# Decoder of two layers: where the second layer's cross attention gets its tables and first contexts, and the order of two short chains beside it

## The reference, cut to what matters

```python
x = x + L0_attn(ln(x))            # 16 heads, relative bias
x = x + L0_xattn(ln(x), ctx, ctx) # block structured here
x = x + L0_ffn(ln(x))             # 8 experts, two chosen per token, capacity 896 each
x = x + L1_attn(ln(x))            # running sums over the sequence, exp(clip(.)) weights
x = x + L1_xattn(ln(x), ctx)      # 16 heads of 8, rotary, 1500 keys, softmax
x = x + L1_ffn(ln(x))             # 8 routed experts + a shared one
```

```python
logits = xt @ Wg
idx1, idx2 = argmax(gates), argmax(logits without idx1)
pos1 = cumsum(mask1) - mask1, pos2 = cumsum(mask2) - mask2 + sum(mask1)
xe[idx, pos] += xt                                  # dispatch
h = gelu(xe @ W1 + b1); ye = h @ W2 + b2            # experts
out = ye[idx1, pos1] * w1 + ye[idx2, pos2] * w2     # combine
```

## Time and profile before

| | |
|---|---|
| median of three runs | 1534.07 us |
| the profiled execution | 1527.03 us |
| its span in the trace | 1525.2 us |
| TensorE busy | 1358.7 us, 89% |
| VectorE busy | 1093.6 us, 72% |
| ScalarE busy | 821.8 us, 54% |
| POOL busy | 825.7 us, 54% |
| mean granted TensorE clock | 0.951 |
| moved by DMA | 134.71 MB, mean 88 GB/s |

### The profile page before, as it was taken

The page is one execution under the profiler, slowest core; times in us unless marked ns, Lnnn a source line. Parts: engine busy times, 40 slices in busy tenths (PEclk is TensorE's granted clock), DMA queues, the critical chain, the costliest instruction groups (busy, mean ns, idle before and its releaser), DMA issues.

```text
span 1525.2 us, 41823 instructions
## 1 busy us (share of the span) xinstructions
PE 1358.7 (89%) x17179; PEld 927.0 (61%) x17179; DVE 1093.6 (72%) x1832; ACT 821.8 (54%) x1804; POOL 825.7 (54%) x736
## 2 busy tenths in 40 slices
PE   6788999998967996759999999999999999789998
PEld 4567788788935663335666566656665666555554
DVE  6885767656747887747888888888888888435554
ACT  3442334355622331436777777777777777733332
POOL 6665322424654675747778777877787774000000
PEclk9868999999987998779999999999999999989999
DMA  4004400032271034364555554555464554305230
GB/s 128 2 1 128 159 2 2 19 85 86 65 153 39 1 71 78 75 118 124 125 124 133 118 129 123 133 118 132 121 133 118 128 123 93 96 3 111 61 61 13
DMA packets 76511, 134.71 MB, mean 88 GB/s; under 512 B 18017, under 2 KB 56034, under 8 KB 73058
## 3 DMA queue, kind: packets, MB, share of 16 engines
q1 hardware_dynamic: 74274, 127.84, 35.0%
q0 software_dynamic: 2048, 4.20, 1.0%
HBM read 100.54 MB, written 34.73 MB: 89 GB/s over the span
## 4 chain that ended last, share of the span: by engine, by line
PE 35%; POOL 12%; ACT 8%; issue 3%; DVE 3%; DMA 1%; SPq 0%; ACTq 0%; POOLq 0%; DVEq 0%
PE ps L2158 8%; POOL ARENA L2362 8%; PE ps L916 7%; PE ps L2142 5%; POOL ARENA L2368 4%; PE ps L928 4%; PE ps L2105 3%; ACT ARENA L2312 3%; PE ps L2096 2%; ACT ARENA L2290 2%; PE ps L2119 2%; ACT ARENA L2303 2%; ACT ARENA L2296 1%; PE ps L2167 1%; DVE ARENA L2232 1%
## 5 line engine op out<-in xcount | busy, mean ns | idle before, releaser
L2232 DVE TENSOR_REDUCE ARENA<-ps 112x2 f32<-112x1000 f32 x384 | 456.4, 1197 | 122.6 <-PE ps L2119 119.8
L2312 ACT ACTIVATE ARENA<-ps 125x448 f32<-125x448 f32 x768 | 378.4, 549 | 129.0 <-PE ps L2142 128.4
L2362 POOL TENSOR_TENSOR ARENA<-ARENA 64x500 f32<-64x500 f32 x192 | 264.6, 1378 | 106.4 <-ACT ARENA L2290 88.2
L2142 PEld LDWEIGHTS ps<-ARENA 64*125 64x125 bf16 x3072 | 122.9, 134 | 134.6 <-ACT ARENA L2312 70.7
L2142 PE MATMUL ps<-ARENA 64*125 64x112 bf16 x3072 | 169.6, 229 | 19.9 <-ACT ARENA L2312 18.7
L2158 PE MATMUL ps<-ARENA 125*17 125x112 f32 x6144 | 185.5, 261 | 0.0
L2119 PE MATMUL ps<-ARENA 64*112 64x500 bf16 x768 | 153.4, 388 | 9.8 <-DVE ARENA L2232 9.4
L127 POOL TENSOR_TENSOR rs<-rs,mhalf 128x1 f32<-128x1 f32 x96 | 71.7, 750 | 161.1 <-DVE rs L122 160.8
L2158 PEld LDWEIGHTS ps<-ARENA 125*17 125x17 f32 x6144 | 136.7, 97 | 32.1 <-issue 21.9
L2368 POOL TENSOR_TENSOR ARENA<-ARENA 128x500 f32<-128x500 f32 x96 | 147.1, 1533 | 8.1 <-DVE ARENA L2225 0.7
L2373 POOL TENSOR_TENSOR ARENA<-ARENA 128x500 bf16<-128x500 f32 x96 | 111.0, 1157 | 37.7 <-ACT ARENA L2296 37.7
(11 more groups left out here) (273 smaller groups left out, 2384.7 us busy)
## 6 DMA issues: line engine op xcount, KB each, us to landing
ARENA<-key_parts SPq DMA_DIRECT2D x192, 187.5 KB, 3.9
ARENA<-in_ctxT SPq DMA_DIRECT2D x96, 250.0 KB, 3.7
key_parts<-ARENA SPq DMA_DIRECT2D x64, 375.0 KB, 2.6
ARENA<-token_weights SPq DMA_DIRECT2D x16, 512.0 KB, 5.3
slots<-in_c_blank SPq DMA_DIRECT2D x2, 1472.0 KB, 12.5
results<-ARENA SPq DMA_DIRECT2D x42, 64.0 KB, 1.6
ARENA<-in_L_ffn_W SPq DMA_DIRECT2D x1, 2048.0 KB, 8.7
ARENA<-in_L_ffn_W SPq DMA_DIRECT2D x4, 512.0 KB, 10.1
```

Of the source, the lines that this page charges most:

```text
L2142: m = e.matmul(ps[0:KT, b1[h], 112 * g:112 * g + 112], KS[b % 4][r, g, KT * kt:KT * kt + KT], Q1[r, b % 2, 112 * g:112 * g + 112], start=T ...
L2232: e.tensor_reduce(mxp[0:112, b % 2, 2 * g:2 * g + 2, ch], ps[0:112, b1:b1 + 2, 0:500], AX, ALU.max) \
L2312: e.activation(Pb[0:KT, n % NP_, 448 * h:448 * h + 448], ps[0:KT, b1[h], 0:448], ACT.Exp, bias=0.0, scale=1.0).then_inc(exped.sem, 1)
L2362: e.tensor_tensor(T2[r:r + 64, :], T0[64 - r:128 - r, n % 2, :], sin[64 - r:128 - r, sl], ALU.mult) \
```

## The change

Five things change. The long attention's four projection tables, its cosine and sine in three pieces each, and the six pieces of contexts 0 and 1 are issued by SP inside the expert stage, one behind each of the first 16 results. Its other loads (context 2, output weights, the small tables, ones and zeros) are issued in the L1 self-attention once all gathers have landed. For this the arrays of the long attention are laid out anew: contexts, projection tables, cosine and sine between the words of the expert stage and those of the self-attention, context 2 in the last words of the expert stage, and the last stage's arrays begin at the same place. The signal for the early tables (`c0_in`) is apart from that for the rest. On POOL the late norms' powers of a step go to the step's beginning, ahead of its product and its gathers. The second chunk's routing gets a PSUM bank of its own (4), `route` is split (tiles 8 to 14 at expert tile 2, tile 15 at expert tile 3) and goes ahead of `down`, `count` goes ahead of `down` at expert tile 6, and the VectorE parts and the exponential of the gates move one expert tile or more up.

```diff
@@ -1025,6 +1025,7 @@
             REC, NW = 1156, 5
+            R_BANK = (5, 4)
             NI = sum(SLOTS)
...
@@ -1126,37 +1127,44 @@
             def sp(e, w):
+                ahead = stages[4].parts["ahead"]
                 for i in range(NI):
...
                     e.dma_start(YS[c][128 * k:128 * k + 128], Y[:, i % 8]).then_inc(y_out[i % 8].sem, 16)
+                    if i < len(ahead):
+                        ahead[i](e, w)
                     if i == SLOTS[0] - 5:
...
 
-            def route(e, w, c):
+            def route(e, w, c, lo, hi):
+                bk = R_BANK[c]
                 w.wait_ge(*f0_in(len(loads)))
-                w.wait_ge(*free[5])
-                for t in range(*SPLIT[c]):
+                if lo == SPLIT[c][0]:
+                    w.wait_ge(*free[bk])
+                for t in range(lo, hi):
                     w.wait_ge(*ln_out(2, t))
                     n = 8 * (t - SPLIT[c][0])
-                    m = e.matmul(ps[:, 5, n:n + 8], xT[:, 128 * t:128 * t + 128], wg, start=True, stop=True)
-                m.then_inc(routed.sem, 1)
-                free[5] = sel(NSEL * c + 1)
+                    m = e.matmul(ps[:, bk, n:n + 8], xT[:, 128 * t:128 * t + 128], wg, start=True, stop=True)
+                if hi == SPLIT[c][1]:
+                    m.then_inc(routed.sem, 1)
+                free[bk] = sel(NSEL * c + 1)
 
...
                 T = SPLIT[c][1] - SPLIT[c][0]
-                cnt = ps[:, 5, 0:16 * T + 16].rearrange("p (t n) -> p t n", n=16)
+                bk = R_BANK[c]
+                cnt = ps[:, bk, 0:16 * T + 16].rearrange("p (t n) -> p t n", n=16)
                 w.wait_ge(*ones_set(3 + len(Mb) - 1))
...
                 w.wait_ge(*sel(NSEL * c + 14))
-                w.wait_ge(*free[5])
+                w.wait_ge(*free[bk])
                 e.matmul(cnt, trib, Mb[c], start=True, stop=False, skip_group_check=True)
...
                 m.then_inc(counted.sem, 1)
-                free[5] = sel(NSEL * c + 15)
+                free[bk] = sel(NSEL * c + 15)
 
...
@@ -1217,15 +1225,17 @@
                         up(e, w, i)
+                    if i == 2:
+                        route(e, w, 1, SPLIT[1][0], NT - 1)
+                    if i == 3:
+                        route(e, w, 1, NT - 1, NT)
+                    if i == 6:
+                        count(e, w, 1)
                     down(e, w, i - 1)
...
                         ln_turn(e, w, 2, NT - 1, 5, free)
-                    if i == 3:
-                        route(e, w, 1)
-                    if i == 6:
-                        count(e, w, 1)
                     if i in norm_at:
...
@@ -1432,17 +1442,19 @@
             def dve(e, w):
-                steps = {4: ("logits", "first", "second"), 6: ("counts", "bases", "slots"), 7: ("table",), 8: ("gates",), 9: ("shares",)}
+                steps = {3: ("logits", "first", "second"), 4: ("counts", "bases"), 6: ("table",), 7: ("gates",), 8: ("shares",)}
                 for i in range(1, NI + 1):
...
                         ln_scale(e, w, 2, NT - 1)
+                    if i == 5:
+                        choose(e, w, 1, "slots")
                     if i - 2 + NW < NI and i > 1:
...
                         choose(e, w, 1, part)
-                    if i in (10, 11):
-                        keep(e, w, i - 10)
+                    if i in (9, 10):
+                        keep(e, w, i - 9)
                     if i + 1 in norm_at:
...
@@ -1496,7 +1508,7 @@
                         ln_copy(e, w, 2, NT - 1, 5)
-                    if i == 5:
+                    if i == 4:
                         gate(e, w, 1)
...
@@ -1540,7 +1552,7 @@
                          early_pool=early_pool, sp=sp, pe=pe, dve=dve, act=act, pool=pool, gather=gather, combine=combine,
-                         combined=combined,
+                         combined=combined, late=lambda: [g(4) for g in gathered], words=place["used"],
                          end=lambda: [y_cp(NI), down_mm(NI), gated(4 * NI), kept(11), w_cp(NI)] + chunk_out(1))
...
@@ -1786,6 +1798,9 @@
                         stages[2].parts["gather"](e, w, u)
+                    for u in LATE_NORM.get(t - 1, ()):
+                        ln_power(e, w, 3, u)
+                        between.append(ln(INV, 3, u))
                     stages[4].parts["early_pool"](e, w, t, ("total",))
...
@@ -1796,9 +1811,6 @@
                     for u in late[2:] if t == 0 else late:
                         stages[2].parts["gather"](e, w, u)
-                    for u in LATE_NORM.get(t - 1, ()):
-                        ln_power(e, w, 3, u)
-                        between.append(ln(INV, 3, u))
                     if t >= 3:
                         ln_power(e, w, 4, t - 3)
...
@@ -1829,6 +1838,14 @@
             Qh, Ql = mem(TP, BF16), mem(TP, BF16)
+            passing = stages[2].parts["words"] - SK
+            assert place["used"] <= passing
+            place["used"] = passing
+            C = [mem(SK) for _ in range(3)]
+            C = [C[1], C[2], C[0]]
+            wq, wqr, wk, wv = (mem(128) for _ in range(4))
+            cos, sin = mem(SK), mem(SK)
+            assert place["used"] <= ARENA_WORDS - stages[3].parts["words"]
             KSb, Vb = slots(1), values_of(1)
...
@@ -1846,11 +1863,13 @@
             p = "L1_xattn_"
-            loads = [(wq, a[p + "WqT"]), (wqr, a[p + "WqRT"]), (wk, a[p + "WkT"]), (wv, a[p + "WvT"]), (wo, a[p + "WoT"]),
-                     (hm, a["c_own"]), (cos, a["c_cos"]), (sin, a["c_sin"]), (cq, a["c_cosq"]), (sq, a["c_sinq"])]
+            tables = [(wk, a[p + "WkT"]), (wv, a[p + "WvT"]), (wq, a[p + "WqT"]), (wqr, a[p + "WqRT"])]
+            tables += [(v[:, 500 * ch:500 * ch + 500], a[n][:, 500 * ch:500 * ch + 500])
+                       for ch in range(3) for v, n in ((cos, "c_cos"), (sin, "c_sin"))]
+            loads = [(wo, a[p + "WoT"]), (hm, a["c_own"]), (cq, a["c_cosq"]), (sq, a["c_sinq"])]
             ones = lambda dst, r: (dst[r:r + 16].rearrange("p i g k -> p (i g k)"), a["c_ones"][:, 0:dst.shape[1] * 4 * SK])
             loads += [x for r in (48, 112) for x in (ones(KSa, r), (QS[r:r + 16].rearrange("p g n -> p (g n)"), a["c_zero"]))]
-            c1_in, c2_in = signal("c1_in", len(loads), 16), signal("c2_in", 2, 16)
+            c0_in, c1_in, c2_in = signal("c0_in", len(tables), 16), signal("c1_in", len(loads), 16), signal("c2_in", 2, 16)
             qs_in = [signal("qs_in%d" % i, 6, 16) for i in range(2)]
...
@@ -2001,14 +2020,23 @@
                 sl = slice(500 * ch, 500 * ch + 500)
-                e.dma_start(C[:, b % 3, sl], a["ctxT"][b][:, sl]).then_inc(ctx_in[b % 3].sem, 16)
+                e.dma_start(C[b % 3][:, sl], a["ctxT"][b][:, sl]).then_inc(ctx_in[b % 3].sem, 16)
 
             def load(e, w):
+                for mark in stages[2].parts["late"]():
+                    w.wait_ge(*mark)
+                for ch in range(3):
+                    fetch(e, 2, ch)
                 for dst, src in loads:
                     e.dma_start(dst, src).then_inc(c1_in.sem, 16)
-                for b in range(3):
-                    for ch in range(3):
-                        fetch(e, b, ch)
+
+            def load_table(i):
+                return lambda e, w: e.dma_start(*tables[i]).then_inc(c0_in.sem, 16)
+
+            def load_context(b, ch):
+                return lambda e, w: fetch(e, b, ch)
+
+            ahead = [load_context(b, ch) for b in range(2) for ch in range(3)] + [load_table(i) for i in range(len(tables))]
 
...
@@ -2189,7 +2217,7 @@
                 for step in early(t):
-                    w.wait_ge(*c1_in(len(loads)))
+                    w.wait_ge(*c0_in(len(tables)))
                     pe_step(e, w, step)
...
@@ -2487,7 +2516,7 @@
         for k, f in enumerate((l0_attn, l0_xattn, l0_ffn, l1_attn, l1_xattn, l1_ffn)):
-            place.update(used=642 if k == 5 else 0, low=k % 2 == 0 or k == 5)
+            place.update(used=stages[4].parts["passing"] if k == 5 else 0, low=k % 2 == 0 or k == 5)
             stages.append(f())
```

More of the change, by code:

```diff
@@ L2396, in early_pool @@
                         pool_step(e, w, step)
[L2398 removed]
+            return Stage(load=load, ahead=ahead, passing=passing, chore_pool=chore_pool, between=between, early_sp=early_sp, early_pe=early_pe, early_dve=early_dve,
                          early_act=early_act, early_pool=early_pool, sp=sp, pe=pe, dve=dve, act=act, pool=pool,
```

19 lines of the change are left out of this document (8 added, 11 removed).

## The result

| | before | after |
|---|---|---|
| median (lowest to highest), four runs each | 1536.97 us (1530.72 to 1545.25) | 1512.95 us (1509.65 to 1516.68) |
| ratio, 95% interval | | 0.9863 [0.9818, 0.9908] |
| the profiled execution, its span | 1527.03, 1525.2 us | 1509.65, 1507.9 us |
| mean granted TensorE clock | 0.951 | 0.959 |
| moved by DMA | 134.71 MB | 134.71 MB |

The forecast was 1519 us (1510 to 1531), a gain of 14.8. Measured on the profiled executions it is 17.4; the ratio makes 21 of 1534 (14 to 28).

What follows compares the result with a forecast made beforehand. TensorE and VectorE were taken as starved at the seam to the L1 self-attention by late gathers and POOL's order, and TensorE by late second-chunk slots. 11.5 + 3.3 = 14.8 us off the 1534.07 median gave 1519 us, range 1510 to 1531.

Steps and rivals of the forecast that it cites:

- Part 1: Long attention's loads moved between expert results: cost on the path 0, bounds 0 and 13.3 us, DMA share 0.51.
- Part 2: L1 self-attention: late norms' powers ahead of POOL's gathers, together with the moved loads; gain 11.5 us.
- two corrections: On the 11.7 us gain at the self-attention: 1.2 us off for slower gathers on POOL, 1.0 added for TensorE's clock.
- The clock term: Self-attention step 4, 10.35 us with TensorE at half clock in it: 1.0 us gained, bounds 0 and 2.8.
- Part 3: Expert layer, second chunk's routing one tile earlier: indices 2.3 us sooner, clock worth 1.0; gain 3.3 us, bounds 1.3 and 3.9.
- rival B: TensorE's clock holds both in the self-attention and at the second chunk's turn: gain 21, 1513 us; chance 0.12.
- C: Expert layer: the moved load pieces make scatters land 6.6 us late, turn at 382.8; gain 7.5, 1526 us; chance 0.14.
- D: POOL itself is the limit, gathers and scatters lengthened under a busy VectorE: gain 6, 1528 us; chance 0.05.
- E: The DMA jam moves into the expert layer, slots come 25 us late: 16 slower, 1550 us; chance 0.06.
- The reason for summing the parts once: Self-attention: moved loads and reordered powers were summed once, at 11.5 us, because each alone would give little.

Runs made afterwards that it cites:

- powers_and_chain: Kernel before with late norms' powers ahead on POOL and the second routing chain earlier, loads not moved; 1511.37 us, ratio 0.9851.
- changed_again: The changed kernel run once more, nothing altered; ratio 0.9892 against the kernel before.
- powers_mid: The changed kernel with each pair of late powers one step earlier still, between the step's two gathers; 1515.7 us, ratio 0.9880.
- loads_only: Kernel before with only the long attention's loads moved and the arrays laid out anew; 1534.27 us, ratio 0.9981.
- chain_only: Kernel before with only the second chunk's routing chain one expert tile earlier; 1524.52 us, ratio 0.9954.
- contexts_late: Kernel before with only the nine context pieces issued once all gathers have landed; 1535.69 us, one run.
- powers alone: Kernel before with only the late norms' powers moved to the step's beginning on POOL; 1525.46 us, ratio 0.9955.
- ones_late: Kernel before with only the loads of ones and zeros issued once all gathers have landed; 1535.54 us, one run.

## Why the prediction was right, point by point

**Part 1 at nothing on the path: right for the path, wrong for its use.** The pieces cost nothing visible in after; scatters' issue and slots' load kept their lengths (27.1 us from indices to turn, 27.6 before). The window carried more than the 0.51 forecast, 0.69: the 3.3 MB of pieces make 83 of the 121 GB/s more, and the rest is traffic that came earlier into the window, which the working had left at 84. But its use in the ramp was 0.7 to 1.4 us, not the 6.10 wait that it removed, and nothing against the jammed traces with 40.25; in the whole time powers_and_chain is faster without it. Whether the pieces set the phase of the last scatters is open: the slow phase came in two of five profiled executions with pieces and the new chain (changed_again, powers_mid), and in none of the three with the chain and no pieces.

**Part 2: right, with luck in its two corrections.** U of step 2 was put 7.2 us behind that of step 1 and came 6.99 behind; U of step 4 was put near 31 and came at 31.33. Without its two corrections the working had 29.9, so 1.4 us came on top where 1.2 was taken, but not as it was thought. The gathers' median hardly moved (0.957 us against 0.952). But one of them, at 436.12, took 1.80 us instead of 0.99: it began beside VectorE's product, itself held up by POOL's, and ended 0.86 us behind that product's end at 437.06. The pair of powers at 451.17 took 1.79 instead of 1.10 beside VectorE's sum of 450.79. By the reading of the Trainium skill (SBUF — State Buffer, Practical consequences) in the prediction, two-input products of VectorE don't touch the gathers' descriptor writing, and the correction would be near 0. The trace doesn't agree with that for the gather at 436.12; whether its descriptor writing was held up or its reading of the indices can't be told. For the powers, which read SBUF, the trace agrees with the page. VectorE's own delay behind POOL (1.3 us at 443.04) moves U of step 3 and not U of step 4, since POOL goes on without it.

The clock term is right in number and not in mechanism. Taken was 1.0 for the half clock in step 4. That step went from 10.35 to 9.70 us, 0.65 less, at a clock of 0.82 instead of 0.72; over the other kernels it took 9.8 to 11.3, so no run shows what the clock alone gave. The other 1.0 came in step 5 to 6, at full clock before and after: 7.49 us became 6.47. The prediction calls the old one undisturbed, but VectorE stood there for POOL's powers too (before):

```profile
492.75 0.35 DVE L143 TENSOR_SCALAR xn<-XR,mv,rs 128x128 f32<-128x128 f32 x1 [1.66 <-POOL rs L127]
```

All nine kernels with the new order on POOL have 6.46 to 6.51 here, loads_only, chain_only and contexts_late 7.48 to 7.49. So 11.5 was taken for the ramp with what follows it and 12.0 came, by one term that fell short and one that the working lacked: that they nearly made up the 1.0 is luck.

**Part 3: mechanism right, size too small; this is the term that was mis-sized.** Taken 3.3, bounds up to 3.9, measured 5.1. The logits came 2.3 us sooner, as put, 0.9 behind the first result's issue instead of 3.2. The rest of the chain was said to keep its length and became 0.77 shorter, 7.40 for 8.17: one weight copy of 0.75 lies in it where two did. And the clock was taken at 1.0 between 0 and 1.6; with the stand at 0.8 to 1.0 us it held in every run, and the stretch to U of step 0 became 1.5 to 1.7 shorter. In the runs with a stand of 2.74 it fell. So half of rival B came true, at this one place. That the whole item from first load to indices (3.1) fits so well with the chain's own 2.3 and 0.8 is partly luck, since the item scatters by more than 1 us.

**The sum.** 14.8 taken, 17.1 of the change's own measured, 17.4 in the profiled executions, 17 and 21 by the two ratios. The case of forecast and rival B together (faster by 1%) came out; the ratio's 21 is rival B's own number, and its interval takes in 14.8 too. C, D and E did not come out. D had its point, though: POOL's chain ends last in the ramp of after.

**The reason for summing the parts once** fell: powers alone gave 9.3 of 10.3 us in the ramp, so the first part was hardly needed there.

## What to carry to other kernels

Before moving a late transfer, ask what the waiter would wait for next: removing a wait of 6.10 us was worth 1.4 at most, and the order of a few short operations on POOL was worth 8 to 9. Look at a wait in more than one trace before pricing it: this one was 3.15 us in another kernel that left its stretch alone. Send loads like the ones and zeros here, few partitions and long rows, when nothing small is due beside them. A TensorE stand costs more than its length: in the nine traces with a stand of 2.7 us or more before the turn, the way from there to U of step 0 took 52.5 to 53.8 us, in the five with 0.8 to 1.0 it took 50.9 to 51.1.

## What the runs showed of the hardware

POOL's product and these operations of VectorE don't run beside each other. U of step 2 takes 3.18 us from 433.88 to 437.06, where it takes 1.22 alone, and POOL's product runs from 434.05 to 435.96, so it is 1.96 us longer beside a product of 1.91. The same at 443.04 (the second of two scales ends 0.35 us behind the product's end at 445.38) and at 452.96 (0.34 behind 454.83). The Trainium skill (SBUF — State Buffer, 🔬 SBUF: two separate sides) calls it an exclusive lock on a shared pair of ports, held for the whole instruction; the rows agree in this. The page gives the pair to whichever starts first; at 433.88 VectorE's record starts 0.17 us before POOL's, and it is VectorE's that gets longer, so who goes first can't be read from the starts.

A scatter takes POOL 0.96 us where it meets none of VectorE's weight copies and up to 1.49 where each one meets a copy (changed_again, above).

By the Trainium skill (DMA: Bandwidth & Descriptors, Queues, rings and completion order) an engine takes its queues in turn, so a full SP queue should hold a gather up little. That fits ones_late better (a gather took 6.4 us at most beside 379 GB/s) than the narrow loads, where one took 14.9 to 16.1. The measurement decides: what stands in the other queue matters, and beside the narrow loads the longest gather took 9 to 10 us more.
